# Row list read ahead of the rows' weights, and one hidden unit of the shared layer computed inside the experts' steps

## The chip, the cores and the metric

One core of a Trainium2 chip. The metric is the device time of the whole program in microseconds (us); lower is better. Times are given as the median of several executions; views of the profile come from one profiled execution.

## The reference

One block of a graph model on 1250 rows of 512 numbers, in float32. The rows are normalised; a graph attention over 40,000 edges and a linear attention are added; then comes a mixture of experts:

```python
h = _ln(x, ln1_g, ln1_b).reshape(T, D)
logits = (h @ Wr) @ codebook.T / TEMP
vals, idx = jax.lax.top_k(jax.nn.softmax(logits), 2)      # 2 of 64 experts
w = vals / jnp.sum(vals, axis=-1, keepdims=True)
eh = jax.nn.silu(jnp.einsum('td,edf->tef', h, W1) + b1)   # 512 -> 256
eo = jnp.einsum('tef,efd->ted', eh, W2) + b2              # 256 -> 512
moe = jnp.einsum('te,ted->td', combine, eo)               # combine holds w
shared = (jax.nn.silu(h @ Ws1 + bs1) @ Ws2 + bs2) * 0.25  # 512 -> 1024 -> 512
```

and behind it a normalisation and a last layer (512 -> 256 -> 512). The change lies in the mixture alone: in the end of the router and in where the shared layer's work stands.

## The kernel before

**Stages.** The program is written by hand, engine by engine, with semaphores. Up to about 545 us it does the attentions and the router; from 545 to 795 us the experts; then the last layer. All weights of the experts (W1 and W2 of 64 experts, blocks repeated for large experts) come from HBM during the experts' stage, 512 KB a piece, on SyncE's queue.

**The router's end.** VectorE finds each row's two experts, ranks the rows of each expert and writes one-hot tables (`slots`, `rowhot`). TensorE multiplies them into the `list` bank (L1809). VectorE meanwhile makes the two weights of each row (`wtop`), spreads them over the 64 experts (`prob` and `tmpr`, L1141 and L1142), adds them (L1144), takes them times 4 (L1146) and raises `comb_made`. Only then does it read the `list` bank (L1168 to L1172) and make `gat` (L1174), whose semaphore `gat_made` lets GpSimd start the first two gathers of rows (`Zg`, L648). TensorE waits for `comb_made` before it transposes `prob` (L1816); ScalarE copies that to `combT`, which is only the left operand of a product with `b2_s` (L1759) in the shared layer.

**The shared layer** is cut in parts that fill TensorE's time. `hidden` unit i (0 to 19) is a piece of `silu(h @ Ws1)`: 250 rows by 256 hidden columns, in two halves of 8 matmul instructions each (L1748); ScalarE applies Silu (L1401). `shared` t (0 to 9) is one 125-row tile of the second product, in three thirds of 6 instructions (L1759, L1762); VectorE adds it to `HM`. Units 0 to 6 stand in the router, to fill waits. Unit 7 stands between the transposes of `prob` and the experts. The rest is dealt out over the experts' steps by `parts_beside`, by a cost for each part and a share for each step, and is fixed when the program is built (`BESIDE`).

**The experts' steps** are 28: `QUADS` = 7 quads of four experts (32 rows each), then 21 pairs (64 rows each). In step q of the quads TensorE does: the hidden product (`quad_hidden`, L1847, needs W1 of the step and `hgT`), the first part of `BESIDE[q]`, two transposes of `eh` (L1882), the four transposes of the rows of step q+2 (L1837, needs gather q+2), the other parts, and the result product (`quad_result`, L1858, needs W2 of the step). In a pair step p: the hidden product (L1874), the result of step p-1 (L1892), the parts, the transposes.

**The weights' queue.** SyncE issues W1 of step q+1 when the hidden product of step q is done, and W2 of step q+1 when the result of step q is done, strictly in that order (L502 and L505), because a quad fills all four buffers. So W1 of a quad stands in the queue behind W2 of the quad before it. In the pairs, W2 of step p+1 and W1 of step p+2 are issued one behind the other when the result of step p-1 is done.

```python
def quad_weights(q):
    e = owners(4 * q)
    at_least(sp, h_done, q)
    for j in range(4):
        first_weights(e[j], j)
    at_least(sp, e_done, q)
    for j in range(4):
        second_weights(e[j], j)
```

PSUM banks are taken in turn by a plan written out (`TURNS`); in the experts' stage the parts alternate between banks 6 and 7.

Of the kernel before, what the change touches and what calls it, by code (L numbers as in the profile page):

```python
# [12 lines left out]
ALU = mybir.AluOpType  # L13
# [41 lines left out]
class Turns:  # L55
# [63 lines left out]
    ("hidden", ["act"]),  # L119
    ("combT", ["act"] * 3),  # L120
]), (2, 6, [
    ("hidden", ["act"]), ("shared", ["dve"] * 2),
    ("hidden", ["act"] * 4), ("shared", ["dve"] * 2), ("fb", ["dve"]),
    ("hidden", ["act"] * 4), ("shared", ["dve"] * 2),
    ("hidden", ["act"] * 4), ("shared", ["dve"] * 4),
]), (8, 0, [
# [30 lines left out]
def parts_beside():  # L157

    parts = []
    for c, first in enumerate((8, 8, 12, 16)):  # L160
        if c:
            parts += [("hidden", i, k) for i in range(first, first + 4) for k in range(2)]
        parts += [("shared", t, k) for t in (2 * c, 2 * c + 1) for k in range(3)]
        if c == 1:
            parts += [("fb", 0, k) for k in range(2)]
    cost = {"hidden": 4 * 250, "shared": 3 * 512, "fb": 530}
    share = [4 if p < QUADS else 1.4 for p in range(PAIRS0)]
    total, done, table, p = sum(cost[p[0]] for p in parts), 0, [[] for _ in range(PAIRS0)], 0
    for part in parts:
        while p < PAIRS0 - 1 and done >= total * sum(share[:p + 1]) / sum(share):  # L170
            p += 1
        table[p].append(part)
        done += cost[part[0]]
    return table


BESIDE = parts_beside()


# [6 lines left out]
def block_kernel(nc, A, out):  # L186
    ctx = ExitStack()
    with ctx:
# [6 lines left out]
        def sem(name):  # L195
            return ctx.enter_context(nc.semaphore(name))
# [45 lines left out]
        def ph(name, shape, dt, kb):  # L242

            return at(name, shape, dt, G + kb * KB)
# [60 lines left out]
        prob = ph("prob", [P, T, E], F32, 40)  # L305
# [3 lines left out]
        tmpr = ph("tmpr", [P, T, E], F32, 49)  # L309
# [53 lines left out]
        def bank(b, n, p=128, off=0):  # L363
            return ps[0:p, b * 512 + off:b * 512 + off + n]

        def set_of(n):


            i, s = divmod(n, T)
            return i, s, i // 3, *THIRDS[i % 3]  # L370
# [46 lines left out]
        comb_made, slots_made = sem("comb_made"), sem("slots_made")  # L417
# [14 lines left out]
        def col(name, i, n=1, p=128):  # L432
            o = COLS[name][0] + i
            return cols[0:p, o:o + n]
# [263 lines left out]
        def _(v):  # L698
            V_ = nc.vector

            def reads(name, i):
                v.wait_ge(filled, TURNS.filled(name, i))
# [269 lines left out]
            for n in range(SETS * T):  # L972
                i, s, pair, o, w = set_of(n)
# [167 lines left out]
            V_.tensor_tensor(prob[:, :, :], M1[:, :, :], wtop[:, :, 0:1].to_broadcast([P, T, E]), ALU.mult)  # L1141
            V_.tensor_tensor(tmpr[:, :, :], M2[:, :, :], wtop[:, :, 1:2].to_broadcast([P, T, E]), ALU.mult)  # L1142
            v.drain()
            V_.tensor_tensor(prob[:, :, :], prob[:, :, :], tmpr[:, :, :], ALU.add)  # L1144
            v.drain()
            V_.tensor_scalar(prob[:, :, :], prob[:, :, :], 4.0, None, ALU.mult)  # L1146
            v.drain().then_inc(comb_made, 1)


            def shared_sum(t):  # L1150
# [22 lines left out]
            v.drain()  # L1173
            V_.tensor_single_scalar(gat[:, :], lst[:, :], 1, ALU.logical_shift_right)  # L1174
            v.drain().then_inc(gat_made, 1)
            def fold_last():
                reads("fb", 0)
                V_.tensor_tensor(bf1F[:, :], bank(TURNS.bank("fb", 0), 2), col("bf1", 0, 2), ALU.add).then_inc(dve_read, 1)
                for k in range(KD):
                    V_.tensor_scalar(Wf1_s[:, k, :], Wf1_s[:, k, :], col("gf", k), None, ALU.mult)  # L1180
                v.drain().then_inc(f1_folded, 1)

            def parts_read(parts):
                for name, t, part in parts:
                    if name == "shared" and part == 2:
                        shared_sum(t)
                    if name == "fb" and part == 1:
                        fold_last()
# [3 lines left out]
            for p in range(PAIRS0):  # L1192
                hidden_kept(p, p % 2)
                k = 1 if p < QUADS else len(BESIDE[p])
# [57 lines left out]
        def _(a):  # L1252
            S_ = nc.scalar

            def reads(name, i):
                a.wait_ge(filled, TURNS.filled(name, i))
# [80 lines left out]
            for n in range(SETS * T):  # L1337
                i, s, pair, o, w = set_of(n)
# [50 lines left out]
            for k in range(KD):  # L1389
                i = S_.activation(hT[:, k, 0:500], hT[:, k, 0:500], ACT.Identity, bias=col("b1ln", k), scale=col("g1", k))  # L1390
# [4 lines left out]
            def shared_hidden(i):  # L1395
                c, g = divmod(i, 4)
                if c >= 2 and g == 0:
                    a.wait_ge(filled, TURNS.filled("shared", 2 * c - 3))
                reads("hidden", i)
                for k in range(2):  # L1400
                    j = S_.activation(hsT[:, c % 2, 2 * g + k, :], bank(TURNS.bank("hidden", i), 250, 128, 250 * k), ACT.Silu, bias=col("bs1", 2 * g + k))  # L1401
                j.then_inc(act_read, 1)
# [6 lines left out]
            for c, tiles in enumerate(((0, 4), (4, 4), (8, 2))):  # L1409
                reads("combT", c)  # L1410
                S_.copy(combT[:, tiles[0] * P:(tiles[0] + tiles[1]) * P], bank(TURNS.bank("combT", c), tiles[1] * P, E)).then_inc(act_read, 1)
            shared_hidden(7)

            def quad_turned(q, u):
                a.wait_ge(x_done, q + 1)
# [93 lines left out]
        def _(pe):  # L1509
# [10 lines left out]
            def read_by_now(name, i):  # L1520
                who, count = TURNS.group_read(name, i)
                pe.wait_ge(act_read if who == "act" else dve_read, count)
# [27 lines left out]
            for c, (o, n) in enumerate(CHUNKS):  # L1550
# [3 lines left out]
                for m in range(KD):  # L1554
# [3 lines left out]
                    for k in range(KD):  # L1558
                        i = MM(bank(b, n), mW[:, 0, k, m * 128:m * 128 + 128], xnT[:, k, o:o + n], start=k == 0, stop=k == KD - 1)  # L1559
# [15 lines left out]
            for t in range(T):  # L1575
                for w in range(2):
# [3 lines left out]
                    for k in range(KD):  # L1580
                        i = MM(bank(b, D, P), xnT[:, k, t * P:t * P + P], mW[:, 1 + w, k, :], start=k == 0, stop=k == KD - 1)  # L1581
# [10 lines left out]
            for k in range(KD):  # L1592
                i = MM(bank(b, 1, E), Wr_s[:, k, :], col("b1ln", k), start=k == 0, stop=k == KD - 1)
# [14 lines left out]
            for t in range(T):  # L1608
                for i in range(2):
                    b = turn("mix_o", 2 * t + i)  # L1610
                    for j in range(2):
                        k = MM(bank(b, 130, P, 130 * j), qT[:, 2 * i + j, t * P:t * P + P], kvb[:, 2 * i + j, :], start=True, stop=True)
                    k.then_inc(filled, 1)
            for t in range(T):
                read_by_now("mix_o", 2 * t + 1)
                b = turn("moT", t)
                for k in range(KD):
                    i = nc.tensor.transpose(bank(b, P, 128, k * P), mo[:, t, k * 128:k * 128 + 128], ident[0:P, 0:P])
                i.then_inc(filled, 1)
            pe.wait_ge(mwo_in, 16)  # L1620
            for t in range(T):
                read_by_now("moT", t)
                b = turn("mix_wo", t)
                for k in range(KD):
                    i = MM(bank(b, D, P), moT[:, k, t * P:t * P + P], mWo[:, k, :], start=k == 0, stop=k == KD - 1)  # L1625
# [22 lines left out]
            for u in range(30):  # L1648
                t, part = divmod(u, 3)
                b = turn("cT", u)  # L1650
                for j in range((4, 4, 2)[part]):
                    i = nc.tensor.transpose(bank(b, 128, P, 128 * j), Cx[:, 4 * part + j, P * t:P * t + P], ident[:, :])
# [45 lines left out]
            for c, (o, n) in enumerate(CHUNKS):  # L1698
                if c == 1:
                    pe.wait_ge(head_kept, SETS)  # L1700
                for m in range(KD):
                    b = turn("gnn_a", KD * c + m)
                    for k in range(2):
                        i = MM(bank(b, n), Wa_s[:, k, m:D:KD], aggT[:, k, o:o + n], start=k == 0, stop=k == 1)  # L1704
# [3 lines left out]
                for t in range(o // P, (o + n) // P):  # L1708
                    b = turn("gnn_f", t)
                    for k in range(KD):  # L1710
                        if t == o // P:
                            read_by_now("gnn_a", KD * c + k)
                        i = MM(bank(b, D, P), h1T[:, k, t * P:t * P + P], Wf_s[:, k, :], start=k == 0, stop=k == KD - 1)  # L1713
# [18 lines left out]
            for c in range(2):  # L1732
                b = turn("logit", c)
                for t in range(5):
                    i = MM(bank(b, E, P, t * E), rTs[:, (5 * c + t) * P:(5 * c + t + 1) * P], cbT_s[:, :], start=True, stop=True)
# [6 lines left out]
            def shared_hidden(i, half):  # L1742
                c, g = divmod(i, 4)
                if i == 8 and half == 0:
                    pe.wait_ge(hT_scaled2, KD)
                b = turn("hidden", i) if half == 0 else TURNS.bank("hidden", i)
                for k in range(KD):
                    j = MM(bank(b, 250, 128, 250 * half), Ws1_s[:, k, (2 * g + half) * 128:(2 * g + half + 1) * 128],  # L1748
                           hT[:, k, c * 250:c * 250 + 250], start=k == 0, stop=k == KD - 1)
                if half:  # L1750
                    j.then_inc(filled, 1)
# [14 lines left out]
            def whole_hidden(i):  # L1766
                for half in range(2):
                    shared_hidden(i, half)
# [5 lines left out]
            for q in range(T):  # L1774
                i = MM(bank(b, 1, E), Mb[:, q, :], ones[:, 0:1], start=q == 0, stop=q == T - 1)
# [25 lines left out]
            for m in range(2):  # L1801
                i = MM(bank(b, NB_MAX, 128, (1 + m) * NB_MAX), b1_s[:, m:DFF:2], mine[:, :], start=True, stop=True)
# [5 lines left out]
            for n in range(TOPK * T):  # L1808
                i = MM(bank(b, 3 * NP), rowhot[:, n, :], slots[:, n, :, :].rearrange("p s q -> p (s q)"), start=n == 0, stop=n == TOPK * T - 1)  # L1809
# [3 lines left out]
            for c, (t0, n) in enumerate(((0, 4), (4, 4), (8, 2))):  # L1813
                b = turn("combT", c)
                for t in range(n):
                    i = nc.tensor.transpose(bank(b, P, E, t * P), prob[:, t0 + t, :], ident[0:P, 0:P])  # L1816
                i.then_inc(filled, 1)
            whole_hidden(7)
            read_by_now("combT", 2)
            read_by_now("hidden", 6)  # L1820
            read_by_now("list", 0)
# [193 lines left out]
```

## Time and profile before

| | us |
|---|---|
| median of 3 runs (864.43 to 867.04) | 865.0 |
| the profiled execution | 865.03 |
| its span, first to last instruction | 863.3 |
| TensorE busy | 817.0 |
| VectorE busy | 502.3 |
| ScalarE busy | 282.8 |
| GpSimd busy | 137.0 |

The profiled execution's own time is the median's, so sums can be made against either. 1.7 us lie outside the span. Busy shares are averages over stages with different limits: what ends a wait in the stretch in question counts, not the share.

### The profile page before, as it was taken

The numbers are of one execution on the slowest core, as the hardware profiler recorded it, in microseconds if no ns is written. First come the engines' busy times: TensorE is split into PE (matmuls) and PEld (weight loads), VectorE is DVE, ScalarE is ACT, GpSimd is POOL, SyncE is SP. The second block draws the span as 40 slices with busy tenths as digits, with TensorE's granted clock in tenths as the row PEclk, the third lists the DMA queues.
The fourth block names the chain that finished last, engine by engine and source line by source line (L and its number), as shares of the span: only waits on it lengthen the run. The fifth ranks groups of instructions, "written<-read, shape, count | busy, mean of one in ns | idle before, by whom it ended". The sixth has DMA issues, their size and how long they took to land.

```text
span 863.3 us, 11681 instructions
## 1 busy us (share of the span) xinstructions
PE 817.0 (95%) x3910; PEld 476.0 (55%) x3910; DVE 502.3 (58%) x1293; ACT 282.8 (33%) x549; POOL 137.0 (16%) x159
## 2 busy tenths in 40 slices
PE   4999999999999999999999999989898999999897
PEld 2565555754568544444445678546365456644464
DVE  7687667666686899999956568210112222222652
ACT  4631111200213666666523442212122222223373
POOL 5100000600100000000000130222223322222230
PEclk9999999999999999999999988999999999999989
DMA  9410000000236540501022335497979999996913
GB/s 261 191 49 1 1 1 1 1 0 1 119 120 135 129 104 17 119 1 49 1 98 58 105 106 196 165 347 283 377 262 355 337 342 344 357 311 211 235 31 95
DMA packets 39482, 127.68 MB, mean 148 GB/s; under 512 B 7049, under 2 KB 7491, under 8 KB 38783
## 3 DMA queue, kind: packets, MB, share of 16 engines
q1 hardware_dynamic: 32379, 108.66, 38.4%
q0 software_dynamic: 6592, 17.93, 5.6%
q8 instruction: 32, 0.52, 0.2%
q10 hardware_dynamic: 452, 0.34, 0.2%
q14 instruction: 27, 0.22, 0.1%
HBM read 114.29 MB, written 17.58 MB: 153 GB/s over the span
## 4 chain that ended last, share of the span: by engine, by line
PE 66%; DVE 11%; DMA 8%; issue 5%; DVEq 4%; SPq 2%; ACT 2%; ACTq 0%; POOL 0%; POOLq 0%
PE ps L1581 8%; DMA W<-in_W 7%; PE ps L1748 7%; DVE att L977 6%; PE ps L1762 5%; PE ps L1559 4%; PE ps L1625 4%; PE ps L1713 4%; PE ps L1874 4%; PE ps L1633 4%; PE ps L1892 4%; PE ps L1540 3%; PE ps L1676 3%; PE ps L1704 2%; PE ps L1955 2%
## 5 line engine op out<-in xcount | busy, mean ns | idle before, releaser
L977 DVE TENSOR_TENSOR att<-es,C 125x832 f32<-125x832 f32 (+1 forms) x120 | 116.3, 1012 | 4.9 <-ACT es L1342 4.2
L1342 ACT ACTIVATE es<-ps 125x832 f32<-125x832 f32 (+1 forms) x120 | 95.4, 867 | 54.9 <-PE ps L1665 54.1
L1676 PE MATMUL ps<-att,V 125*64 125x416 f32 (+1 forms) x480 | 96.7, 525 | 5.6 <-DVE att L977 4.4
L1158 DVE TENSOR_SCALAR hgT<-ps,cols 128x128 f32<-128x128 f32 x120 | 40.9, 405 | 103.9 <-PE ps L1837 103.9
L1748 PE MATMUL ps<-hT,Ws_s 128*128 128x250 f32 x320 | 75.9, 393 | 0.4 <-issue 0.4
L1762 PE MATMUL ps<-Ws_s,hsT 128*125 128x512 f32 x160 | 74.3, 604 | 0.0
L1581 PE MATMUL ps<-mW,xnT 128*125 128x512 f32 x160 | 72.2, 594 | 0.0
L1748 PEld LDWEIGHTS ps<-hT,Ws_s 128*128 128x128 f32 x320 | 62.1, 199 | 16.1 <-issue 8.8
L800 DVE TENSOR_SCALAR ohB<-iotaW,key 125x200 bf16<-125x200 f16 x320 | 65.1, 271 | 0.0
L1676 PEld LDWEIGHTS ps<-att,V 125*64 125x64 f32 x480 | 29.1, 136 | 56.2 <-issue 32.1
L1665 PE MATMUL ps<-Qst,Kst 128*125 128x416 f32 (+1 forms) x240 | 56.9, 370 | 2.0 <-DMA Qst<-qk_d 0.8
L1665 PEld LDWEIGHTS ps<-Qst,Kst 128*125 128x125 f32 x240 | 41.2, 185 | 28.9 <-ACT es L1342 17.8
L1762 PEld LDWEIGHTS ps<-Ws_s,hsT 128*125 128x125 f32 x160 | 28.2, 187 | 42.0 <-issue 42.0
L1164 DVE COPY eh<-ps 128x256 f32<-128x256 f32 x28 | 11.9, 425 | 63.8 <-PE ps L1847 41.5
L1437 ACT COPY eo<-ps 128x512 f32<-128x512 f32 x28 | 16.4, 586 | 96.4 <-PE ps L1892 67.3
L653 POOL DMA_INDIRECT y_d<-eo,lst x27 | 27.5, 1018 | 118.1 <-ACT eo L1437 118.1
L804 DVE TENSOR_TENSOR Cx<-Cx,ps 128x200 f32 x80 | 28.8, 360 | 29.5 <-PE ps L1540 16.8
L648 POOL DMA_INDIRECT Zg<-z_d,gat x30 | 31.0, 1032 | 94.1 <-PE ps L1837 60.9
L1540 PEld LDWEIGHTS ps<-ohB,ohA 125*128 125x128 bf16 x320 | 30.6, 113 | 26.5 <-issue 23.8
L1874 PE MATMUL ps<-W,hgT 128*64 128x256 f32 x336 | 40.9, 385 | 4.5 <-DMA W<-in_W 4.3
L1581 PEld LDWEIGHTS ps<-mW,xnT 128*125 128x125 f32 x160 | 28.4, 188 | 29.0 <-issue 29.0
L610 POOL DMA_DIRECT2D z_d<-yz x10 | 5.5, 548 | 235.9 <-DVE yz L1012 235.7
(282 smaller groups left out, 1237.7 us busy)
## 6 DMA issues: line engine op xcount, KB each, us to landing
W<-in_W SPq DMA_DIRECT2D x140, 512.0 KB, 6.7
Kst<-qk_d SPq DMA_DIRECT2D x32, 156.2 KB, 5.5
Qst<-qk_d SPq DMA_DIRECT2D x32, 156.2 KB, 5.7
Yt<-y_d SPq DMA_DIRECT2D x10, 448.0 KB
Ws_s<-in_Ws SPq DMA_DIRECT2D x2, 2048.0 KB, 9.8
qk_d<-qk_hi POOLq DMA_DIRECT2D x4, 625.0 KB, 3.6
qk_d<-qk_lo POOLq DMA_DIRECT2D x4, 625.0 KB, 4.8
z_d<-yz POOLq DMA_DIRECT2D x10, 250.0 KB, 2.7
```

The costliest lines, as they stand in the source:

```text
L800: i = V_.tensor_scalar(ohB[:, s, j, :], iotaW[:, :], key[:, bass.ds(k + j, 1)], None, ALU.is_equal)
L977: V_.tensor_tensor(att[:, n % AB, :, 0:w], es[:, n % EB, :, 0:w], C[:, s, o:o + w].unsqueeze(1).to_broadcast([P, 2, w]), ALU.mult).then_in ...
L1158: i = V_.tensor_scalar(hgT[:, u, k, :], bank(u, 128, 128, k * 128), col("g1", k), col("b1ln", k), ALU.mult, ALU.add)
L1342: S_.activation(es[:, n % EB, :, 0:w], scores_of(n, w), ACT.Exp, scale=float(DK) ** -0.5).then_inc(s_exp, 1)
L1540: i = MM(bank(b, WN), ohA[:, s, :, j], ohB[:, s, j, :], start=j == 0, stop=j == EG - 1)
L1559: i = MM(bank(b, n), mW[:, 0, k, m * 128:m * 128 + 128], xnT[:, k, o:o + n], start=k == 0, stop=k == KD - 1)
L1581: i = MM(bank(b, D, P), xnT[:, k, t * P:t * P + P], mW[:, 1 + w, k, :], start=k == 0, stop=k == KD - 1)
L1665: k = MM(scores_of(n, w)[:, j, :], Kst[:, h % 4, s * P:s * P + P], Qst[:, h % 4, o:o + w], start=True, stop=True)
L1676: k = MM(sums_of(i, 64 * j, 64, w), V[:, s, pair, j:j + 2, :], att[:, n % AB, j, 0:w], start=s == 0, stop=s == T - 1, skip_group_check=True)
L1748: j = MM(bank(b, 250, 128, 250 * half), Ws1_s[:, k, (2 * g + half) * 128:(2 * g + half + 1) * 128], hT[:, k, c * 250:c * 250 + 250], start ...
L1762: i = MM(bank(b, D, P), hsT[:, t // 2 % 2, k, (t % 2) * P:(t % 2) * P + P], Ws2_s[:, k, :], start=False, stop=k == DSH // 128 - 1)
L1874: i = MM(bank(2, DFF, 128, DFF * u)[R * j:R * j + R], hgT[:, u, k, R * j:R * j + R], W1[2 * u + j][:, k, :], start=k == 0, stop=k == KD - ...
```

## The change

Three things. (1) VectorE reads the `list` bank and raises `gat_made` right after L1142; the sum and the multiplication by 4 of `prob` (L1144, L1146), and `comb_made`, come behind it. (2) The hidden unit 7 no longer stands between the transposes of `prob` and the first step of the experts, on TensorE and on ScalarE. (3) It joins the parts that are dealt out over the steps. The dealing is redone with it, so later parts move too; the banks' plan follows.

```diff
-    ("hidden", ["act"]), ("shared", ["dve"] * 2),
-    ("hidden", ["act"] * 4), ("shared", ["dve"] * 2), ("fb", ["dve"]),
+    ("shared", ["dve"] * 2),
+    ("hidden", ["act"] * 5), ("shared", ["dve"] * 2), ("fb", ["dve"]),
...
-    for c, first in enumerate((8, 8, 12, 16)):
-        if c:
-            parts += [("hidden", i, k) for i in range(first, first + 4) for k in range(2)]
+    for c, own in enumerate(((), range(7, 12), range(12, 16), range(16, 20))):
+        parts += [("hidden", i, k) for i in own for k in range(2)]
...
             V_.tensor_tensor(tmpr[:, :, :], M2[:, :, :], wtop[:, :, 1:2].to_broadcast([P, T, E]), ALU.mult)
             v.drain()
-            V_.tensor_tensor(prob[:, :, :], prob[:, :, :], tmpr[:, :, :], ALU.add)
-            v.drain()
-            V_.tensor_scalar(prob[:, :, :], prob[:, :, :], 4.0, None, ALU.mult)
-            v.drain().then_inc(comb_made, 1)
...
             V_.tensor_single_scalar(gat[:, :], lst[:, :], 1, ALU.logical_shift_right)
             v.drain().then_inc(gat_made, 1)
+            V_.tensor_tensor(prob[:, :, :], prob[:, :, :], tmpr[:, :, :], ALU.add)
+            v.drain()
+            V_.tensor_scalar(prob[:, :, :], prob[:, :, :], 4.0, None, ALU.mult)
+            v.drain().then_inc(comb_made, 1)
...
-            shared_hidden(7)
...
-            whole_hidden(7)
```

The parts of each step, worked out from `parts_beside` (h7a is the first half of hidden unit 7, s2c the third third of tile 2, fb two small products for the last layer):

| step | before | after |
|---|---|---|
| 0, 1 | s0abc; s1abc | the same |
| 2 | h8ab h9ab | h7ab h8ab h9a |
| 3 | h10ab h11ab s2a | h9b h10ab h11a |
| 4 | s2b s2c | h11b s2a s2b |
| 5 | s3abc | s2c s3ab |
| 6 | fb h12ab h13a | s3c fb h12ab |
| 7, 8, 9 | h13b h14a; h14b; h15ab | h13ab; h14a; h14b h15a |
| 10 to 15 | s4a; s4b; s4c; s5a; s5b; s5c | h15b; s4a; s4b; s4c; s5ab; s5c |
| 16 to 21 | h16a; h16b h17a; h17b; h18ab; h19a; h19b s6a | h16a; h16b; h17ab; h18a; h18b h19a; h19b |
| 22 to 27 | s6b; s6c; s7a; s7b; s7c; none | s6a; s6b; s6c; s7a; s7b; s7c |

## Rows read from the trace of the kernel before

**Rows 1.** The page, part 1: busy us, share, instructions.
```profile
PE 817.0 (95%) x3910; PEld 476.0 (55%) x3910; DVE 502.3 (58%) x1293; ACT 282.8 (33%) x549; POOL 137.0 (16%) x159
```

**Rows 2.** Timeline of the router's end: start, us, engine, line, operation, count, [idle before].
```profile
534.42 1.34 PE L1809 MATMUL ps<-slots,rowhot 125*128 125x132 bf16 x20
...
535.45 0.83 DVE L1144 TENSOR_TENSOR prob<-prob,tmpr 125x640 f32<-125x640 f32 x1
...
536.35 0.49 DVE L1146 TENSOR_SCALAR prob<-prob 125x640 f32<-125x640 f32 x1
536.96 0.20 DVE L1168 TENSOR_SCALAR lf<-ps 128x44 f32<-128x44 f32 x1
...
538.90 1.19 POOL L648 DMA_INDIRECT Zg<-z_d,gat  x1 [28.32 <-DVEq L1175]
539.02 1.23 PE L1816 MATMUL ps<-ident,prob 125*64 125x125 f32 x10
...
539.95 1.29 ACT L1411 COPY combT<-ps 64x500 f32<-64x500 f32 x3
...
540.09 3.54 PE L1748 MATMUL ps<-hT,Ws_s 128*128 128x250 f32 x16
540.39 1.03 POOL L648 DMA_INDIRECT Zg<-z_d,gat  x1 [0.30 <-issue]
...
544.14 2.64 DVE L1158 TENSOR_SCALAR hgT<-ps,cols 128x128 f32<-128x128 f32 x8 [6.14 <-PE ps L1837]
...
545.56 1.93 PE L1847 MATMUL ps<-W,hgT 128*32 128x256 f32 x32 [0.98 <-DVE hgT L1158]
```

**Rows 3.** DMA issues at 538.9 us, then 540.4 us: last column us to landing.
```profile
Zg<-z_d,gat POOLq DMA_INDIRECT x1, 3.5
...
Zg<-z_d,gat POOLq DMA_INDIRECT x1, 3.2
```

**Rows 4.** Timeline of TensorE: hidden products of steps 2, 4, 5, 6, 8.
```profile
574.14 3.34 PE L1847 MATMUL ps<-W,hgT 128*32 128x256 f32 x32 [3.56 <-DMA W<-in_W]
...
602.13 1.93 PE L1847 MATMUL ps<-W,hgT 128*32 128x256 f32 x32 [0.70 <-DMA W<-in_W]
...
615.66 3.50 PE L1847 MATMUL ps<-W,hgT 128*32 128x256 f32 x32 [3.65 <-DMA W<-in_W]
...
629.65 1.91 PE L1847 MATMUL ps<-W,hgT 128*32 128x256 f32 x32
...
650.93 1.95 PE L1874 MATMUL ps<-W,hgT 128*64 128x256 f32 x16 [2.55 <-DMA W<-in_W]
```

**Rows 5.** Timeline of SyncE's queue: W2 issued as results 2, 3, 4 end.
```profile
587.29 1.77 SPq L505 DMA_DIRECT2D W<-in_W  x4
...
601.49 2.06 SPq L505 DMA_DIRECT2D W<-in_W  x4
...
612.05 1.76 SPq L505 DMA_DIRECT2D W<-in_W  x4
```

**Rows 6.** Chain that ended last: last W1 transfers of steps 4, 5, 8; start, us.
```profile
591.11 10.89 DMA W<-in_W
...
605.80 9.72 DMA W<-in_W
...
642.83 7.97 DMA W<-in_W
```

**Rows 7.** Busy by stretches: us, five engines, granted clock (PEclk), DMA share, GB/s.
```profile
616.00:618.00 2.00, 2.00 (x24) 1.11 (x20) 0.00 (x0) 0.00 (x0) 0.00 (x0) 0.50 1.02 404
...
650.00:652.00 2.00, 1.06 (x10) 0.92 (x12) 0.00 (x0) 0.00 (x0) 0.19 (x1) 1.00 1.02 418
```

**Rows 8.** TensorE's waits from 655 to 792 us: total, times, longest.
```profile
PE ps L1874 <- DMA W<-in_W: 0.9, 2, 0.7
```

**Rows 9.** Timeline, 634 us: a gather's issue beside VectorE's work in SBUF.
```profile
634.17 1.04 POOL L648 DMA_INDIRECT Zg<-z_d,gat  x1 [0.56 <-issue]
...
634.78 1.29 DVE L1180 TENSOR_SCALAR Wf_s<-Wf_s,cols 128x256 f32<-128x256 f32 x4
```

## The prediction

> **What bounds the kernel now.** I read the page first: TensorE is busy for 95% of the span [rows 1], so a change that only moves its work can win nothing but waits of TensorE. Then the timeline around the moved lines: at the router's end TensorE runs without a gap from the list product (534.42) through the transposes of prob (539.02) and hidden unit 7 (540.09 to 543.63) and is still at unit 7 when the first rows land [rows 2, 3]. Last, the timeline of TensorE in the experts' stage. There it waits for weights: 3.56 us before step 2, 0.70 before step 4, 3.65 before step 5, 2.55 before step 8 [rows 4], then 0.9 us in all over the pairs [rows 8]. Step 6 starts without a wait [rows 4]. So the quads are paced by a loop through SyncE's queue (result done, W2 out, then W1 behind it, then the next hidden product), and the pairs from step 8 on by TensorE.
>
> **Part 1, the list first.** VectorE's sum and product (0.83 and 0.49 us) with their drains fill 535.45 to 536.96, where the list is read [rows 2]. The list product ends at 534.42 + 1.34 = 535.76, so the reading can start at about 535.86, with 0.1 us for the semaphore: 1.1 us earlier (at most 1.2, because the list isn't there before 535.76; at least 0.9). The first gather is then issued at 538.90 - 1.1 = 537.8 and lands 3.5 us on, at 541.3; the second at 539.3, landing 3.2 us on, at 542.5 [rows 2, 3]. Behind it comb_made comes at about 535.86 + 1.1 (four short operations, one every 0.28 us) + 1.5 = 538.5. TensorE wants it at 539.02, after unit 6. The cover is 0.5 us; without it each tenth late would be a tenth on TensorE. Cost taken: nothing.
>
> A price from the notes, which the sum does without: the Trainium skill (SBUF — State Buffer, the "DVE blocks DMA" trap) says that GpSimd can't write the descriptors of its DMAs while VectorE runs a two-port operation from SBUF to SBUF. The nearest row speaks of it: a gather's issue that ran beside such a multiplication took 1.04 us [rows 9], against 1.03 for one without [rows 2]. By the rule the first gather would be late by up to the 0.49 us of L1146; by the row, by 0.01. I take the row and keep the other in the range.
>
> **Part 2, unit 7 leaves the router.** It gives back 3.54 us of TensorE [rows 2], but not 3.54 us of time: what is late next is the first gather (541.3) and the copies to combT (539.95 + 1.29 = 541.24) [rows 2]. Transposes of step 0 at 541.4. Before, hgT began 0.51 us behind the end of unit 7 (544.14 - 543.63) and one step's half of its 2.64 us is 1.32 [rows 2]: now 541.4 + 0.5 + 1.3 = 543.2. The second rows land at 542.5, and their transposes take as long as the first rows', 0.5 with 0.1 to start: 543.1. So the first hidden product starts at about 543.4, with 0.1 to 0.2 for semaphores, not 545.56: 2.15 us earlier. ScalarE's two Silus of unit 7 go too; it was waiting there anyway.
>
> **Part 3, unit 7 in the steps.** Half a unit is 3.54 / 2 = 1.77 us [rows 2]. By the table of parts:
> - A third of a shared tile has 6 instructions of 512 columns where a unit has 16 of 250 in 3.54 us, so it takes some 3.54 x 3072 / 4000 = 2.7 us, a tile's first one, with the b2 product, about 2.9.
> - Steps 0 and 1 are as before, so W2 and W1 for step 2 are issued 2.15 earlier and step 2 starts at 574.14 - 2.15 = 572.0, again after a wait of about 3.6 us. It has one half more: result 2 ends 0.4 earlier than before (-2.15 + 1.77), at 586.9, not 587.29 [rows 5].
> - W1 of step 4 stands behind W2 of step 3, issued there. Before, it took from 587.29 to 591.11 + 10.89 = 602.0, 14.7 us [rows 5, 6]: now 601.6. Step 3 has four halves as before but no third, 2.9 us less, so its result ends at 601.4 - 0.4 - 2.9 = 598.2, and TensorE **waits 3.4 us** where it waited 0.70. Step 4 starts 0.4 earlier.
> - Step 4 has a half more and a slightly longer third (+0.2): result 4 ends at 612.05 - 0.4 + 1.95 = 613.6 [rows 5]. W1 of step 5 now has its W2 issued at 598.3, before W1 of step 4 has landed, so the queue doesn't run dry between them. Before, W2 and W1 took 605.80 + 9.72 - 601.49 = 14.0 us from a queue that was empty [rows 5, 6]; less about 2.3 us of issue and landing, they now follow W1 of step 4: 601.6 + 11.8 = 613.4. Step 5 starts at 613.6 without a wait, where it waited 3.65.
> - That removes a second cost. After that wait the granted clock stood at 0.50, 1.2 GHz, and the hidden product took 3.50 us, not 1.93; after the wait of 2.55 the clock was 1.00 [rows 4, 7]. So result 5 is early by 2.1 + 1.6 = 3.7, at 625.9.
> - Step 6 now waits. Its W1 stands behind W2 of step 5, issued at 613.6; with 14.0 to 14.7 us as above it lands at 627.6 to 628.3. I take 628.0: 1.7 earlier than 629.65 [rows 4], after a wait of 2 us. Step 6 has a third for a half, +0.9. Result 6 ends 0.8 earlier, and W1 of step 8 behind it (642.83 + 7.97 = 650.8 before [rows 6]) also: step 8 starts 0.8 earlier, after a wait of some 3.
> - From step 8 to 27 TensorE is the bound, and what is left of the unit's 3.54 us, one half, must be paid: +1.77. The waits of 0.9 us [rows 8] fall at other steps: two short steps in a row (16 and 17, one half each) leave weights that take 8 to 10 us [rows 6] too little time. Estimate 1.5 us in place of 0.9: +0.6; ends 0 and +2.
>
> **The sum**: -0.8 + 1.77 + 0.6 = +1.6 us, at the experts' end and, since the last layer waits for the last result, at the kernel's: 865.03 + 1.6 = 866.6. In short, 2.15 us of early start and the removed wait and slow clock of step 5 are spent on longer waits before 4, 6 and 8 and on 3.54 us of work.
>
> **The rivals.**
> - *More of the stretches at half clock.* Steps 2, 4 and 8 each start after some 3 to 3.6 us of idle TensorE. Between 2.55 us (full clock) and 3.56 (half) [rows 4, 7] no row decides. The sum has one slow stretch, at step 2. With a second, at 4 or 8, it is 1.6 more (3.50 - 1.93): 868.2; with a third 869.8. With none, 865.0. The slow stretch delays a result and with it all transfers behind it. For it: two such gaps before, both slow. Against: both were over 3.5. It decides once the idle time before step 4 passes some 3.5 us. This is how the change ends slower: chance 0.25, at 868.2 or above.
> - *The queue was held by SyncE's order, not by bandwidth.* If W1 lands as soon as 12 us after its W2 (4.2 MB at the 404 to 418 GB/s that full DMA engines moved [rows 7] would take 10.4, and issue and landing come on top), the waits before 4, 6 and 8 are each up to 1.5 shorter, the early start survives, and the end is 3 better: 863.6, and 862.0 where step 2 also stays at full clock. Against: 14.0 and 14.7 us were taken twice [rows 5, 6]. Chance 0.25.
> - *The start doesn't move.* If the gathers don't land earlier or comb_made comes late (the port above, a longer landing), step 0 starts at up to 545.5 and all is 2.1 later: 868.7. It needs over 2 us lost in a stretch whose operations are all seen; half a microsecond of it only shifts the forecast to 867.1. Chance 0.08.
> - The forecast itself, one slow stretch and the waits as above, within about 1.2 us: 865.4 to 867.8, chance 0.42.
>
> **How the numbers follow.** About 0.3%, 2.6 us, is what a measurement can tell from no change: 862.4 to 867.6. Faster needs the second rival nearly whole: 0.19. Slower takes the first rival, the third and the upper edge of the forecast: 0.30. Same 0.51. The range reaches from the second rival's 862.0 to the first one's 869.8.
>
> **What would show it.** The first gather issued about 1.1 us earlier against the list product, and the first hidden product 2.1 us earlier; no wait before step 5 and full clock there; waits of 3.4, 2 and 3 us before steps 4, 6 and 8; the last result 1.6 us later. I am wrong if step 4 starts without a wait (then transfers aren't the bound), if step 8 starts over 2 us early, or if waits in the pairs are above 3 us in sum.

## The result, and the profile after

| | before | changed |
|---|---|---|
| median of 14 runs each | 864.79 | 869.39 us |
| ratio to before, 95% interval | | 1.0054 (1.0036 to 1.0071) |
| profiled execution, its span | 865.03, 863.3 | 870.61, 868.8 us |
| same kernels on another chip (23 and 6 runs) | 864.00 | 873.11 us, 1.0101 (1.0066 to 1.0136) |

A run more than 1.5% above the fastest of its kernel is left out of the ratios and of the fits below (one of the 14 of the changed kernel).

Slower by 4.6 us. The forecast's range, up to 869.8 us, holds the median of this series by 0.4 us; the likeliest case, no change, did not come. The other chip's series, 9.1 us slower, lies above the range.

The router's end after the change, from the timeline (start, us, engine, line, operation, count, [idle before]):

```profile
534.85 1.34 PE L1807 MATMUL ps<-slots,rowhot 125*128 125x132 bf16 x20
...
536.22 0.20 DVE L1163 TENSOR_SCALAR lf<-ps 128x44 f32<-128x44 f32 x1 [0.49 <-PE ps L1807]
...
537.37 0.82 DVE L1171 TENSOR_TENSOR prob<-prob,tmpr 125x640 f32<-125x640 f32 x1
538.15 1.19 POOL L647 DMA_INDIRECT Zg<-z_d,gat  x1 [26.84 <-DVEq L1170]
538.27 0.49 DVE L1173 TENSOR_SCALAR prob<-prob 125x640 f32<-125x640 f32 x1
...
541.72 0.75 PE L1834 MATMUL ps<-ident,Zg 128*128 128x128 f32 x4 [1.04 <-ACT combT L1410]
...
542.82 0.75 PE L1834 MATMUL ps<-ident,Zg 128*128 128x128 f32 x4 [0.36 <-DMA Zg<-z_d,gat]
...
543.92 3.35 PE L1844 MATMUL ps<-W,hgT 128*32 128x256 f32 x32 [0.35 <-DVE hgT L1153]
```

Read it against [rows 2]. The router's end shifts from execution to execution (the list product starts between 532.1 and 535.7 us in the 14 profiles of this document), so starts are counted here from the list product's start. The first gather is issued 538.15 - 534.85 = 3.30 us behind it, where it was 4.48: 1.18 us earlier. The first hidden product starts 9.07 us behind it, not 11.14: 2.07 earlier. But it takes 3.35 us, not 1.93. The stretches of the same place show why (us; busy time of PE, PEld, DVE, ACT, POOL; granted clock; DMA share; GB/s):

```profile
542.00:544.00 2.00, 1.29 (x12) 0.91 (x15) 1.50 (x5) 0.00 (x0) 0.77 (x1) 1.00 0.04 14
544.00:546.00 2.00, 2.00 (x24) 1.08 (x28) 1.15 (x4) 0.00 (x0) 1.25 (x2) 0.57 0.34 94
546.00:548.00 2.00, 2.00 (x14) 0.71 (x6) 0.42 (x1) 0.00 (x0) 0.00 (x0) 0.58 0.27 77
```

Where unit 7 stood, TensorE now idles 1.04, 0.36 and 0.35 us around two short groups of transposes, and right behind it the clock is at its lower level, 1.2 GHz. Steps 2, 4, 5, 6 and 8 of the experts, TensorE's timeline:

```profile
573.10 1.93 PE L1844 MATMUL ps<-W,hgT 128*32 128x256 f32 x32 [2.52 <-DMA W<-in_W]
...
601.19 2.60 PE L1844 MATMUL ps<-W,hgT 128*32 128x256 f32 x32 [3.71 <-DMA W<-in_W]
...
614.56 1.91 PE L1844 MATMUL ps<-W,hgT 128*32 128x256 f32 x32
...
629.82 3.49 PE L1844 MATMUL ps<-W,hgT 128*32 128x256 f32 x32 [2.48 <-DMA W<-in_W]
...
652.81 3.04 PE L1871 MATMUL ps<-W,hgT 128*64 128x256 f32 x16 [2.75 <-DMA W<-in_W]
```

Against [rows 4]: the wait before step 5 is gone, waits before 4, 6 and 8 are there, and all three are followed by slow products (2.60, 3.49, 3.04 us). The forecast's slow product at step 2 did not come: 1.93 us, after a wait of 2.52 us and not 3.6. TensorE's waits from 656 to 800 us, behind step 8's own, and the whole stretch from step 8 to step 27:

```profile
PE ps L1871 <- DMA W<-in_W: 4.3, 5, 1.7
```

```profile
652.81:793.99 141.18, 136.89 (x733) 79.07 (x733) 34.77 (x94) 32.82 (x105) 41.73 (x40) 0.99 0.92 330
```

4.3 us of waits stand against 0.9 [rows 8], and the stretch takes 141.2 us; before, from the start of step 8 [rows 4] to that of step 27 at 788.15, it took 137.2, but the work in the two isn't the same: the stretch now holds half a unit more (1.77 us), and tile 7's last third (2.7 us) stands behind it. So the fair measure is up to the start of the last result. From the list product to there it is 267.1 us, before 259.1. Summed over stretches of 2 us, the experts' stage has some 13.6 us at half clock in this execution, before 6.8; that alone can be up to 3.4 of the 8.0 us. The last layer gave 3 us back in this execution, since before it had a half-clock stretch there (slice 39 of the page's clock row was 8, here it is 9); the second profile of the changed kernel has the 8 too, so this is most likely chance of one execution and no effect of the change.

### The profile page after: what moved, and what is told of

Its sections match the earlier page's. It is cut to its first block, busy times and chain, and to the rows that moved or that the text cites. A ratio compares the mean times of both kernels' runs of the same rounds, so it can differ in the third digit from the quotient of the medians.

```text
span 868.8 us, 11680 instructions
## 1 busy us (share of the span) xinstructions
PE 816.6 (94%) x3910; PEld 476.3 (55%) x3910; DVE 501.9 (58%) x1293; ACT 282.6 (33%) x549; POOL 137.2 (16%) x159
## 4 chain that ended last, share of the span: by engine, by line
PE 59%; DVE 13%; DMA 11%; issue 5%; DVEq 5%; SPq 3%; ACT 2%; POOLq 1%; POOL 0%; ACTq 0%
DMA W<-in_W 9%; PE ps L1579 8%; DVE att L976 6%; PE ps L1746 5%; PE ps L1623 4%; PE ps L1711 4%; PE ps L1631 4%; PE ps L1760 4%; PE ps L1871 4%; PE ps L1889 3%; PE ps L1538 3%; PE ps L1674 3%; PE ps L1702 2%; PE ps L1557 2%; PE ps L1663 2%
```

## The experiments

**How they are compared.** Every run lists its mean granted clock, and time follows it closely. The 102 runs of the kernel before that the comparisons use have medians of 861.8 us at a mean clock of 0.992, 864.5 at 0.988, 866.6 at 0.984. One line for each kernel with a common slope, fitted to 243 runs (these and the runs of all the other kernels), gives 1.34 us for each 0.002 of clock. It splits a kernel's distance from before in two: how much slower it is at the same clock, and what its own mean clock costs. The second part isn't always chance: half clock that the kernel itself brings about, as at step 0, is in it. It is also the less certain one, by ± 0.8 to 1.9 us for each kernel (± 1.0 for the changed one).

| kernel | ratio to before (95%) | at equal clock, us | clock's part, us |
|---|---|---|---|
| changed (both series) | 1.0054 and 1.0101 | +4.2 ± 0.7 | +1.9 |
| e1, list first alone | 1.0000 (0.9972 to 1.0027) | 0.0 ± 0.9 | -0.4 |
| e2, unit moved alone | 1.0074 (1.0048 to 1.0100) | +3.8 ± 1.2 | +1.5 |
| e3, warm start | 1.0052 (1.0026 to 1.0078) | +3.7 ± 0.9 | +0.1 |
| e4, old dealing | 1.0026 (1.0006 to 1.0047) | +0.2 ± 0.9 | +1.4 |
| e5, level quads | 1.0006 (0.9975 to 1.0036) | +0.5 ± 0.9 | +0.7 |
| e6, pairs redealt | 1.0033 (1.0008 to 1.0059) | +3.3 ± 0.9 | +0.2 |
| e7, work alone | 1.0027 (1.0007 to 1.0046) | +2.0 ± 0.9 | +0.4 |
| e8, half a unit into the pairs | 1.0004 (0.9980 to 1.0028) | +1.1 ± 0.9 | -0.6 |

The edits shown are against the kernel before or the changed kernel, as each heading says; `...` marks lines left out. The theory at the start was **work**: unit 7's 3.54 us are paid in the steps, less what the early start brings. Its rivals: the **clock** at the new start, and the **dealing**, that is the other parts that moved with unit 7.

**e1: the list first, nothing else.** Against the kernel before, whose lines for this sum stood ahead of the list's reading:

```diff
             V_.tensor_single_scalar(gat[:, :], lst[:, :], 1, ALU.logical_shift_right)
             v.drain().then_inc(gat_made, 1)
+            V_.tensor_tensor(prob[:, :, :], prob[:, :, :], tmpr[:, :, :], ALU.add)
+            v.drain()
+            V_.tensor_scalar(prob[:, :, :], prob[:, :, :], 4.0, None, ALU.mult)
+            v.drain().then_inc(comb_made, 1)
...
```

> The kernel before with part 1 alone: the list read first, unit 7 left in the router, the dealing as before. If the forecast's account of the start holds, the first gather is issued 1.1 us earlier against the end of the list product, but TensorE is busy with unit 7 until 3.4 us behind the transposes of prob, so the first hidden product starts at most 0.1 us earlier (it waits for hgT of rows whose transposes start when unit 7 ends): ratio 1.000, within 0.2%. The rival, that VectorE's sum and multiplication beside the gather's descriptors delay it, would show a gather issue longer than 1.19 us and a later first hidden product.

The gather was issued 3.30 us behind the list product's start, and the first hidden product came 11.14 behind it, as in the kernel before to the hundredth. No time: part 1 by itself is hidden behind unit 7. The gather's issue took 1.19 us, as before.

**e2: the unit moved, the list read last.** Against the changed kernel:

```diff
             V_.tensor_tensor(tmpr[:, :, :], M2[:, :, :], wtop[:, :, 1:2].to_broadcast([P, T, E]), ALU.mult)
             v.drain()
+            V_.tensor_tensor(prob[:, :, :], prob[:, :, :], tmpr[:, :, :], ALU.add)
+            v.drain()
+            V_.tensor_scalar(prob[:, :, :], prob[:, :, :], 4.0, None, ALU.mult)
+            v.drain().then_inc(comb_made, 1)
...
```

> The changed kernel with part 1 undone: prob is summed and multiplied first, the list read behind it; unit 7 is in the steps and the dealing is the new one. Gathers then land at 4.1 to 4.2 us behind the end of the router's transposes' start as before, so the first hidden product starts 1.0 to 1.1 us later than in the changed kernel (relative to the end of the list product). If the loss lies in the unit's move, this is slower than before by 4.6 plus up to 1.1 us (ratio 1.005 to 1.007); if it lay in the order on VectorE, it would be back at 1.000. The half-clock stretch at step 0 should be there too, since TensorE idles some 3 us in place of 2.

TensorE's timeline of the start:

```profile
536.68 1.23 PE L1814 MATMUL ps<-ident,prob 125*64 125x125 f32 x10
540.77 1.10 PE L1834 MATMUL ps<-ident,Zg 128*128 128x128 f32 x4 [2.87 <-DMA Zg<-z_d,gat]
```

The first hidden product starts 11.25 us behind the list product, 2.2 later than in the changed kernel, twice what I expected (its transposes were slow too, 1.10 us for 0.65 before): without part 1 the early start is nothing, and it began at half clock. The whole loss is there (3.8 ± 1.2 us at equal clock, the changed kernel 4.2 ± 0.7). So it lies in the unit's move and the dealing that comes with it, and the 2.2 us by which the changed kernel starts earlier are worth nothing at its end that these runs can tell.

**e3: fill the idle time at the start.** Against the changed kernel, with matmuls that nobody reads:

```diff
+            filler(2)
             read_by_now("combT", 2)
...
             transposes(1, 0, 1)
+            filler(1)
```

> The changed kernel plus 12 matmul instructions that nobody reads (8 of 250 columns, some 0.9 us, behind the transposes of prob; 4, some 0.45 us, behind the transposes of step 1's rows), which fill most of the 1.75 us in which TensorE idles there. Theory clock at the start: the hidden product of step 0 takes 1.9 us, not 3.35, step 1 starts 1.2 to 1.6 us earlier than in the changed kernel, and of the 4.6 us up to 1.6 go away (ratio to before 1.003 to 1.004). Theory work: the loss is the unit's 3.54 us in the steps; step 0 may be fast, but the end moves by less than 0.5 us (1.005), because the transfers behind it set the pace.

```profile
541.36 1.01 PE L1818 MATMUL ps<-hT,Ws_s 128*128 128x250 f32 x4
...
542.56 0.75 PE L1839 MATMUL ps<-ident,Zg 128*128 128x128 f32 x4 [0.18 <-ACT combT L1410]
...
543.92 0.75 PE L1839 MATMUL ps<-ident,Zg 128*128 128x128 f32 x4 [0.62 <-DMA Zg<-z_d,gat]
```

With the gap filled the first hidden product took 1.93 us and step 1 started 21.8 us behind the list product, not 23.1: the clock was the cause there, and 1.4 us of it. But step 4 then waited 3.67 us for weights and ran at half clock (3.31 us), and the ratio was 1.0052 against 1.0054 (and 1.0101) of the changed kernel. At equal clock it is half a microsecond better, within the error. But its clock's part is 0.1 where the changed kernel's is 1.9. With both, filling the start gives back 1.3 ± 2.5 us against the changed kernel's first series and 2.3 ± 2.4 against both series: anything from nothing to nearly 5 us. The slow start is real, and since e3 still loses 3.7 us at equal clock, it isn't the main loss; how much of the rest it is stays open.

**e4: the old dealing, unit 7 ahead of step 2's parts.** Against the changed kernel; the lines that restore the loop of the kernel before in `parts_beside` are left out:

```diff
...
+    table[2] = [("hidden", 7, 0), ("hidden", 7, 1)] + table[2]
```

> The changed kernel, but with the old dealing of the parts: unit 7's two halves stand ahead of the other parts of step 2, and no other part moves. Theory dealing: the loss comes from the shifted parts (step 14 with two thirds, then short steps 16, 17, 19, 21 whose weights come late, 4.3 us of waits in the pairs against 0.9), so those waits fall back to about 1 us and the time goes down by 2 to 3 us against the changed kernel (ratio to before 1.001 to 1.003). Theory work: the unit costs its 3.5 us less the early start wherever it stands; ratio 1.004 to 1.006, with step 4's wait short and step 3 long.

The stretch from step 8 to step 27:

```profile
656.62:792.97 136.35, 136.06 (x730) 76.75 (x730) 35.35 (x95) 32.80 (x105) 41.73 (x40) 1.00 0.94 339
```

136.4 us, and no wait for weights in it. The quads carry all 3.5 us and paid in clock: three of their hidden products were slow in this execution (steps 0, 2 and 5, 3.39, 3.36 and 3.64 us). At equal clock the loss falls from 4.2 us to 0.2. So of the changed kernel's loss the part that isn't clock comes with the other parts that moved. The ratio, 1.0026, is still clear of 1: what is left, 1.4 ± 1.3 us, is clock. In the same series e2, which differs from e4 in the dealing and in the order on VectorE alone, took 3.7 ± 2.1 us more in the mean, without any correction for the clock.

**e5: the same with level quads.** Against the changed kernel, the loop of the kernel before restored as in e4:

```diff
...
+    units = [("hidden", i, k) for i in range(7, 12) for k in range(2)]
+    table[2], table[3] = units[:5], units[5:]
+    table[4] = [("shared", 2, k) for k in range(3)]
```

> The changed kernel with another dealing: unit 7 joins the quads, whose parts are levelled (step 2: h7ab h8ab h9a; step 3: h9b h10ab h11ab; step 4: s2abc; step 5: s3abc; step 6: fb h12ab h13a), and the pairs keep the parts of the kernel before. Theory pairs: the pairs from step 8 to 27 take 136 to 137.5 us, as with the old dealing, not 141; then the ratio to before is 1.000 to 1.003, and level quads save a part of the waits of the old dealing (step 3 there was long, then step 4 short). Theory quads: what is paid is paid in the quads, wherever the unit stands; ratio 1.003 to 1.005.

Steps 0 to 8 took 103.9 us with 3.5 us more of work in them, against 108.9 in the changed kernel with 1.8 more, and 105.4 before; waits for weights up to step 8 were 8.5 us, not 11.4 as before:

```profile
543.86:647.80 103.94, 95.42 (x609) 54.93 (x609) 19.73 (x53) 21.43 (x81) 25.70 (x24) 0.99 0.82 306
```

The unit's move is nearly free where its work goes into levelled quads (1.0006; at equal clock 0.5 ± 0.9). That speaks against the forecast's view that +1.77 us must be paid. It doesn't quite shut it out: the forecast's whole sum was +1.6, and the interval reaches 1.4 us (3.1 by the ratio). The expectation for the pairs missed: 136 to 137.5 us from step 8 to 27 were expected, 139.9 came. The old dealing doesn't hold this stretch at 136: the seven profiles that have it (before, e1, e4, e5, e7, and v1 and v2 below) read 136.4 to 140.4 us.

**e6: the kernel before with the changed kernel's pairs.** Against the kernel before; the right side of the last line is left out:

```diff
+BESIDE[6] = [part for part in BESIDE[6] if part != ("hidden", 13, 0)]
+BESIDE[7:] = ...
```

> The kernel before, unit 7 in the router and the list read last, but with the pairs' parts dealt as in the changed kernel: step 6 hands its half of unit 13 to step 7, step 14 has two thirds, steps 16 and 17 one half each, and step 27 has a third where it had nothing. The total of TensorE's work is the same. Theory pairs: this alone costs 2.5 to 4 us (ratio 1.003 to 1.005), steps 8 to 27 taking 139.5 to 141 us with over 2 us of waits for weights. Theory work (the unit's 3.54 us are what is paid): ratio 1.000, within 0.15%.

3.3 us at equal clock, with unit 7 in the router, the list read last and not one instruction more. TensorE's waits behind step 8's own, and where the largest is:

```profile
PE ps L1879 <- DMA W<-in_W: 2.7, 3, 1.7
```

```profile
724.60 1.95 PE L1879 MATMUL ps<-W,hgT 128*64 128x256 f32 x16 [1.75 <-DMA W<-in_W]
```

That is step 18, behind the short steps 16 and 17. In all five profiled executions with this dealing step 18 waits: 0.93 (changed), 1.81 (its second profile), 1.70 (e2), 1.98 (e3), 1.75 us (e6, shown). With the old dealing it waits in one of seven (0.98 us, e1), but then step 17 often does, up to 1.25 us. All waits of steps 9 to 27 together are 4.3, 3.7, 2.8, 2.8 and 2.7 us with the new dealing, mean 3.3, and 0.9, 2.7, 0, 2.0, 1.5, 3.0 and 2.5 with the old, mean 1.8. So the 0.9 us of [rows 8], on which the forecast stood, was a low draw; the new dealing adds some 1.5 us of waits to the 1.77 us of work, which fits e6's 3.3.

The expectation for the stretch from step 8 to 27, 139.5 to 141 us, missed: 137.8 came, since the third in step 27 lies behind it. To the start of the last result it was 145.7 us, before 142.6. In e6's profile 2.8 us more are lost ahead of the pairs, for another reason. Step 5 waits 3.57 us here and 3.65 before, its product starts at 614.21 and 615.66 us, and the parts behind it are the same. But the half clock lasts until about 623 us here, and was over by 619 before (first row e6, second the kernel before):

```profile
620.00:622.00 2.00, 2.00 (x3) 0.93 (x4) 0.00 (x0) 0.00 (x0) 0.00 (x0) 0.50 0.99 365
```

```profile
620.00:622.00 2.00, 2.00 (x6) 0.91 (x6) 0.00 (x0) 0.00 (x0) 0.00 (x0) 1.00 0.86 266
```

This is why single profiles can't weigh a change of 3 us, and runs compared at equal clock can.

**e7: the work alone.** The kernel before with 16 more matmul instructions in step 2 (unit 9 computed twice).

```diff
+                        if i == 9 and part == 0:
+                            for half in range(2):
+                                for k in range(KD):
+                                    MM(bank(turn("hidden", 9) if not half and not k else TURNS.bank("hidden", 9), 250, 128, 250 * half),
+                                       Ws1_s[:, k, (2 + half) * 128:(3 + half) * 128], hT[:, k, 500:750], start=k == 0, stop=k == KD - 1)
```

> The kernel before with 16 more matmul instructions in step 2, a second computation of hidden unit 9 into the same bank, 3.54 us of TensorE; nothing else moves. It prices the unit's work in the quads by itself, without an earlier start. Theory work: the forecast's recurrences give result 2 ending 3.5 us later, step 4 3.5 us later (its weights stand behind that result), hence nearly all of it at the end: +3 to +3.5 us, ratio 1.0035 to 1.004. If waits for weights in the quads can hide work, it is below +1.5 us (1.0017).

```profile
580.54 3.54 PE L1904 MATMUL ps<-hT,Ws_s 128*128 128x250 f32 x16
```

3.54 us of work cost 2.0 us at equal clock (2.3 by the ratio). So uneven quads hide some 1.5 ± 0.9 of it; I had expected 3 to 3.5. Counted in full, the 2.07 us of early start would pay for the rest, but by e2 that start is worth little at the end. Only the sum of the two is measured: e4 and e5 put it at 0.2 and 0.5 us, ± 0.9.

**e8: half a unit from the quads into the pairs.** Against the kernel before:

```diff
+BESIDE[6], BESIDE[7], BESIDE[8] = BESIDE[6][:-1], BESIDE[6][-1:] + BESIDE[7][:-1], BESIDE[7][-1:] + BESIDE[8]
```

> The kernel before with one half of a hidden unit, 1.77 us, handed on from step 6 (the last quad) over step 7 to step 8, and nothing else moved: steps 9 to 27 are dealt as before. It splits what the redealt pairs cost (3.3 us at equal clock): the half unit that leaves the quads, where TensorE waits for weights before steps 7 and 8 anyway, and enters the pairs, against the bunching behind it (two thirds in step 14, short steps 16 and 17, a third in step 27). Theory half: +1.5 to +2 us, ratio 1.0015 to 1.0025, and the rest is bunching. Theory bunching alone: the half is still hidden by the wait before step 8 (2.55 us) and the ratio is 1.000.

1.1 ± 0.9 us at equal clock, between the two theories. It doesn't separate them with certainty. By these two values about a third of e6's 3.3 us is the half unit's place and the rest, 2.1 ± 1.2, the bunching behind it.

**Three versions.** v1: unit 7 stays in the router, its second half behind the transposes of steps 0 and 1, the list first (its lines, as in e1, left out here), the dealing of before.

```diff
-            whole_hidden(7)
+            shared_hidden(7, 0)
             read_by_now("combT", 2)
...
             transposes(1, 0, 1)
+            shared_hidden(7, 1)
```

> A version meant to beat both: the list is read first, the dealing is that of the kernel before, and unit 7 stays in the router but in two halves: the first where it stood, the second behind the transposes of steps 0 and 1, where TensorE waited 0.98 us for hgT. The gathers land early enough (7.9 us behind the start of the list product) for the transposes after the first half. The first hidden product starts 10.3 to 10.5 us behind the start of the list product, not 11.14, at full clock: 0.7 us earlier; the end 0.3 to 0.8 us earlier, ratio 0.999 to 1.000, which the timing can hardly tell.

```profile
541.44 0.63 PE L1837 MATMUL ps<-ident,Zg 128*128 128x128 f32 x4
542.26 0.75 PE L1837 MATMUL ps<-ident,Zg 128*128 128x128 f32 x4 [0.19 <-DMA Zg<-z_d,gat]
542.85 1.85 PE L1748 MATMUL ps<-hT,Ws_s 128*128 128x250 f32 x8
544.63 1.93 PE L1847 MATMUL ps<-W,hgT 128*32 128x256 f32 x32
```

The wait of 0.98 us for hgT is gone, at full clock: 10.55 us behind the list product, 0.59 earlier. Ratio 0.9985 (0.9963 to 1.0007), -0.4 ± 0.9 us at equal clock: better than the changed kernel, not shown to be better than before.

v2 adds level steps 3 and 4 (s2a to step 4):

> The version with unit 7 in two halves in the router and the list read first, plus one dealing step: the first third of tile 2 goes from step 3 to step 4, so that steps 3 and 4 carry 7.0 and 8.2 us, not 9.9 and 5.4. Theory (the loop result, W2, W1, hidden of the quads pays uneven steps twice: a late result holds the queue, a short step then waits for it): the wait before step 5 of some 3.6 us shrinks to under 2 us and with it the half clock there; ratio to before 0.996 to 0.998. If quads are paced by the bytes alone, it equals the version without it, 0.9985.

0.9996 (0.9969 to 1.0024), -0.5 ± 0.9 us at equal clock. Step 5 no longer waited, but step 4 did, 3.78 us, and ran at half clock (3.58 us): the wait moved one step forward. Steps 2 and 8 were slow too (2.94, 3.52). The ratio expected, 0.996 to 0.998, did not come: the claim that levelling helps by itself isn't borne out.

v3 takes two halves out of the pairs into the quads as well (steps 2 to 6: h8ab h9ab h10a; h10b h11ab s2a; s2bc s3a; s3bc fb h12a; h12b h13ab h14a):

> As the last one, but with 3.5 us of hidden halves taken out of the pairs and dealt into the quads, levelled at 8.1 to 8.8 us for steps 2 to 6. Theory: levelled quads take more work into their waits for weights (the changed start with levelled quads had 8.5 us of such waits, not 11.4), and the pairs, paced by TensorE, get shorter by what leaves them, less new waits of up to 2 us because their steps come near the 6.5 us that 2.6 MB take: 1.5 to 3 us faster than before, ratio 0.9965 to 0.998. If the pairs are paced by the transfers instead, they take as long as before and the quads longer: ratio 1.000 to 1.003.

0.9977 (0.9953 to 1.0001), the lowest of all; at equal clock it is -0.1 ± 0.9, so what it may have won is the higher mean clock of its 12 runs (0.9902 against 0.9879). In its profile the stretch from step 8 to 27 took 140.4 us with 3.5 us less work in it, 4.1 us of it waits, and two of its hidden products were slow (3.30 us at step 8, 3.04 at step 21). So the pairs did not get shorter by what left them. That they had met the transfers is the likely reason, not a shown one.

The changed kernel once more:

> The changed kernel itself once more, beside the versions below and the kernel before on one chip. Its first result says 1.0054; the account from the other runs (half a unit and later waits put into the pairs, 3.9 us from step 8 to the last result, and 2 us of early start lost in the quads' loop) says the same: 1.004 to 1.007, with half clock at the first hidden product again.

1.0101 (1.0066 to 1.0136), higher than expected, at a mean clock of 0.983; the first hidden product took 3.40 us again. Its time from step 8 to 27, 140.7 us, and its wait for weights there, 3.7, repeat the first profile.

## Why the prediction was right, and where it was not

The range held the median by 0.4 us, at the edge of the case that the forecast gave 0.25. It is partly luck: the sum had 866.6, the second series lies outside, and of the three signs of being wrong one came true.

- **The start** held: gather 1.18 us earlier (1.1 forecast), hidden product 2.07 earlier (2.15), behind ScalarE's copies to combT and the landing, as said. comb_made's cover held too: the transposes of prob follow unit 6 without a wait. The rule of the Trainium skill (SBUF — State Buffer, the "DVE blocks DMA" trap) was not borne out in this place: L1173 ran from 538.27 beside the gather's issue, and the issue took 1.19 us as in [rows 2]; the first four gathers landed 3.1 to 3.4 us behind their issue, before 3.2 to 3.5. The forecast had taken the row.
- **Missed altogether: half clock at step 0.** The working counted 1.1 us of idle before the transposes and the waits for hgT, and took step 0 at 1.93 us. Of the kernels whose unit 7 left the router, it took 3.35, 3.40, 3.64 (e2), 3.39 (e4) and 3.27 (e5), and 1.93 only where the gap was filled (e3). That returned 1.4 of the 2.07 us at once. By e3 it isn't the main loss at the end; the early steps then wait longer for weights in its profile.
- **The quads' waits** were called well: before steps 4, 5, 6, 8 forecast 3.4, none, 2, some 3 us; measured 3.71, none, 2.48, 2.75. Step 2 was not: forecast some 3.6 us and the sum's one slow product, measured 2.52 and 1.93. What followed the waits was not either: after 2.48 and 2.75 us the products took 3.49 and 3.04, though 2.55 had left full clock in [rows 4, 7]. And in v1 one of 3.59 us was followed by 1.93. The length of the wait alone doesn't tell; the rival's point of decision, "some 3.5 us", is wrong. The rival itself came in: counted from the list product, step 8 is 1.4 us later than before where the sum had it 0.8 earlier, and three of the hidden products ahead of it are slow, where before it were two.
- **The pairs** are the term that came out larger: +1.77 of work and +0.6 of waits, 2.4 us. From the start of step 8 to the last result the profiles with this dealing take 145.7 to 149.1 us, mean 147.8 (changed twice, e2, e3, e6), and those with the old dealing 141.7 to 145.7, mean 143.9 (before, e1, e4, e5, e7, v1, v2): 3.9 us. Part of that is clock: a slow hidden product lies in four of the five and in two of the seven. At equal clock e6 gives 3.3 ± 0.9, whose lower end meets the 2.4. The mechanism was named (steps 16 and 17 too short for the weights of step 18), but it is only 0.93 to 1.98 us of the waits; others stand before steps 14, 20, 21 and 23. Their sum was 2.7 to 4.3 us in place of the 1.5 estimated, and the 0.9 that they were counted against is 1.8 in the mean of seven profiles. "I am wrong if waits in the pairs are above 3 us" came true.
- **Which cause** was misjudged most. The sum read the +1.77 in the pairs as the remainder of unit 7 that "must be paid". It isn't the unit's: e4 and e5 hold the whole unit in the quads and lose nothing certain at equal clock, e6 has it in the router as before and loses 3.3. The loss is the half of unit 13 that the new dealing pushed out of the quads, where TensorE waits anyway, and the bunching behind it.
- **The account by cause**, at equal clock: 3.3 of 4.2 us by the redealt pairs (e6); unit 7 in the quads and its early start together come out even (e4, e5, within 0.9). On top comes the lower mean clock, 1.4 ± 1.3 us in e4 and 1.9 ± 1.0 in the changed kernel, of which the forecast had nothing in its sum and a rival at 0.25. How the clock's part divides between step 0 and later steps stays open, and so does the share of bunching in e6 (e8).

## What to carry to other kernels

When a piece of work is handed to a planner that deals by cumulated shares, every later piece moves too: compare the whole table, step by step, with what bounds each stage, because the pieces that move along can cost more than the one that was meant to. A stage that waits for transfers hides part of the work put into it (e7: 3.54 us cost 2.0), but taking work out of the other stage need not win anything (v3). Light steps in a row are apt to be a wait where transfers are issued two steps ahead. A row of waits read from one profile is one draw: read it in several before a forecast stands on it. Count the idle time that an earlier start creates, and look at the clock behind it.

## What the hardware showed

The mean granted clock goes with most of the scatter between runs of one kernel: the kernel before took a median of 861.8 us at 0.992 (12 runs) and 869.0 at 0.980 (two runs). TensorE fell to 1.2 GHz after a stretch that wasn't one wait but a wait, transposes, and two more short waits (1.04, 0.36, 0.35 us), and stayed at 2.4 GHz after a single wait of 3.59 us in v1. A wait for weights as short as 2.22 us was followed by half clock (v3, step 21: the product took 3.04 us, not 1.95), one of 2.55 in the kernel before wasn't. Behind the wait before step 5, half clock was over by 619 us in the kernel before and lasted until about 623 in e6, with the same parts behind it.
